# Causal attention's last batch in another order, its last rows finished inside cross attention

## What is computed

```python
# causal attention, 16 heads of 32
q, k, v = jnp.split(jnp.einsum('bsd,de->bse', x, Wqkv), 3, axis=-1)
q = _layernorm_scale_only(q, q_ln_scale)
k = _layernorm_scale_only(k, k_ln_scale)
...
scores = jnp.where(causal, NEG_INF, scores)
attn = jax.nn.softmax(scores, axis=-1)
ctx = jnp.einsum('bhst,bthd->bshd', attn, v)
out = jnp.einsum('bsd,de->bse', ctx.reshape(B, S, D_MODEL), out_W)
...
x = _layernorm(x + _L1_attn_ref(...))
# cross attention, 8 heads over the 256 rows, keys and values from ctx_2048
x = _layernorm(x + _L1_xattn_ref(x, ctx_2048, ctx_2048, L1_xattn_gamma))
x = _layernorm(x + _L1_ffn_ref(...))
```

## Time and profile before

| | us |
|---|---|
| median of 3 runs | 1987.14 (1986.0 to 1990.6) |
| the profiled execution | 1987.22 |
| its span, first to last instruction | 1985.4 |

### The profile page before, as it was taken

The page is one execution under the profiler, slowest core; times in us unless marked ns, Lnnn a source line. Parts: engine busy times, 40 slices in busy tenths (PEclk is TensorE's granted clock), DMA queues, the critical chain, the costliest instruction groups (busy, mean ns, idle before and its releaser), DMA issues. The chain is left out here.

```text
span 1985.4 us, 33011 instructions
## 1 busy us (share of the span) xinstructions
PE 1808.2 (91%) x12256; PEld 1482.3 (75%) x12256; DVE 1218.6 (61%) x2266; ACT 936.8 (47%) x2405; POOL 360.0 (18%) x405
## 2 busy tenths in 40 slices
PE   6989999999998799999999996889999679999976
PEld 5878999998896578888888886677777455656554
DVE  3446444444445775555555533688888668887857
ACT  2225333333334443333333322566667569989845
POOL 0000000000003111111112000233333414243225
PEclk9989999999999899999999998999999789999989
DMA  3023000000014231011111002100011556765432
GB/s 109 33 91 101 22 22 22 1 22 22 22 38 122 75 101 48 17 43 48 29 35 40 17 26 91 54 12 33 33 54 43 121 161 168 172 167 152 107 107 85
DMA packets 84125, 132.46 MB, mean 67 GB/s; under 512 B 9384, under 2 KB 25384, under 8 KB 83968
## 3 DMA queue, kind: packets, MB, share of 16 engines
q1 hardware_dynamic: 83968, 130.36, 23.2%
HBM read 75.72 MB, written 21.05 MB: 49 GB/s over the span
## 5 line engine op out<-in xcount | busy, mean ns | idle before, releaser
L2287 DVE TENSOR_REDUCE e_nb<-e_s_ps 128x2 f32<-128x1024 f32 x128 | 155.7, 1217 | 57.3 <-PE e_s_ps L2359 57.3
L2241 ACT ACTIVATE e_p<-e_s_ps,e_nb 128x512 f32<-128x512 f32 x256 | 175.5, 701 | 19.8 <-DVE e_nb L2287 19.5
L1710 ACT ACTIVATE p<-p,nb,rq 128x128 f32<-128x128 f32 (+1 forms) x256 | 136.9, 541 | 92.9 <-DVE nb L1811 92.9
L894 PE MATMUL yp<-ccy,toep 128*128 128x288 f32 x600 | 159.2, 413 | 5.8 <-ACT ccy L876 4.0
L2369 PE MATMUL e_t_ps<-ident,e_p 128*128 128x128 f32 x1024 | 144.4, 277 | 18.6 <-ACT e_pT L2249 9.9
L2369 PEld LDWEIGHTS e_t_ps<-ident,e_p 128*128 128x128 f32 x1024 | 114.1, 141 | 57.1 <-issue 47.5
L80 PE MATMUL q_ps<-a_xt_hi,wq_hi 128*128 128x256 f32 x512 | 151.8, 297 | 4.1 <-DVE wo_lo L112 4.1
L1231 DVE SCALAR_TENSOR_TENSOR hm<-gu_ps,us_col,sg 128x256 f32<-128x256 f32 x88 | 42.3, 481 | 176.9 <-ACT sg L1120 176.9
L82 PE MATMUL q_ps<-a_xt_hi,wq_lo 128*128 128x256 f32 x512 | 146.2, 286 | 0.0
L81 PE MATMUL q_ps<-a_xt_lo,wq_hi 128*128 128x256 f32 x512 | 145.9, 285 | 0.0
L527 ACT ACTIVATE ex<-ex 128x512 f32<-128x512 f32 x64 | 40.5, 632 | 213.9 <-DVE ex L590 213.9
(11 more groups left out here) (316 smaller groups left out, 5190.6 us busy)
## 6 DMA issues: line engine op xcount, KB each, us to landing
x_after<-n_r SPq DMA_DIRECT2D x16, 512.0 KB, 3.0
toep<-padded_kernels SPq DMA_DIRECT2D x32, 256.0 KB, 3.6
qs<-e_xh SPq DMA_DIRECT2D x64, 128.0 KB, 2.5
qs<-e_xl SPq DMA_DIRECT2D x64, 128.0 KB, 2.5
ks<-e_ch SPq DMA_DIRECT2D x64, 128.0 KB, 2.5
ks<-e_cl SPq DMA_DIRECT2D x64, 128.0 KB, 2.5
x<-x_after SPq DMA_DIRECT2D x9, 512.0 KB, 4.6
x<-in_x SPq DMA_DIRECT2D x8, 512.0 KB, 4.0
```

What stands on the lines that cost most here:

```text
L894: last = pe.matmul(yp[:, lo % 2, 0:NCOL], self.toep[h % 2][:, (lo - li) * P:(lo - li + 1) * P], self.ccy(h)[:, li, 0:NCOL], start=(li == 0 ...
L1710: act.activation(p[n % 3][:, h, part[t]], p[n % 3][:, h, part[t]], ACT.Exp, bias=nb[i][:, t, h:h + 1], scale=rq[u][:, t:t + 1], accum_out= ...
L2241: act.activation(pr[i][:, a, :], s_ps[i][:, a, :], ACT.Exp, bias=nb[i][:, a:a + 1], accum_out=sums[t][:, j, q:q + 1]).then_inc(e_done, 1)
L2287: dve.tensor_reduce(nb[i][:], s_ps[i][:], AX.X, ALU.max, negate=True).then_inc(nb_done, 1)
```

## The change

1. c_hi, x_hi and scale_x of FirstBatch move to step 27, c_lo and x_lo to step 28. stack takes a list of heads: heads 0 and 1 are stacked in SP's turn of batch 6, ahead of store(5) and residual(6); heads 2 and 3 in that of batch 7, ahead of store(6).
2. In the last batch ScalarE's two copies (copy_pt) come before exps(n, 0), and VectorE's copy between the first maxima and reciprocals(n - 1, 1). TensorE's order becomes the turns of n - 2, scores(n + 1), values(n - 2). output(6, 0) comes behind values(28), in step 30, ahead of the turns of step 31; output(6, 1) between the turns and the values of step 31.
3. The output of batch 7 is made by group of heads (output_of_group(7, k), 6 matmuls for both halves): group 0 before values(30), group 1 before values(31), groups 2 and 3 behind.
4. The residual of batch 7 is taken from the x tile in SBUF, which is also where the result is made. Residual, statistics, power, apply and store of batch 7 move into cross attention (class LastRows): residual before VectorE's loop, statistics at m = 1, apply at m = 4, power behind GpSimd's first memset, the store on SP behind the load of batch 1; SP waits for it behind the experts' loads.
5. In cross attention the banks e_v_ps and e_m_ps take the places of the two output banks of causal attention, TensorE waits for the residual sums before it first writes them, and turn_context and context of batch 0 move into the loop, to m = 3 and m = 5.

```diff
@@ FirstBatch
-    def stack(self, sp):
+    def stack(self, sp, heads):
         sp.wait_ge(self.xl_done, 1)
         sp.wait_ge(self.cl_done, 1)
-        for j in range(HT):
+        for j in heads:
@@ new class LastRows
+    def bank_read(self, eng, t):
+        eng.wait_ge(self.p_free[t], self.counts[t])
+
+    def residual(self, dve):
+        for t in range(T):
+            dve.wait_ge(self.o_mm, T * B - T + t + 1)
+            dve.tensor_tensor(self.r[:, t, :], self.p_ps[t][:], self.r[:, t, :], ALU.add).then_inc(self.p_free[t], 1)
+
+    def statistics(self, dve):
+        self.norm.statistics(dve, B - 1, [(self.p_free[t], self.counts[t]) for t in range(T)], r=self.r)
...
@@ l1_attention, SP
                         after.load(sp)
+                        after.stack(sp, (0, 1))
                     if b == B - 1:
-                        after.stack(sp)
+                        after.stack(sp, (2, 3))
                     if b:
                         norm.store(sp, b - 1)
+                    if b and b < B - 1:
                         sp.wait_ge(norm.stored, 16 * b)
                         residual(b)
-                norm.store(sp, B - 1)
-                sp.wait_ge(norm.stored, 16 * B)
@@ GpSimd
+                    if n == NG * (B - 1) - 1:
+                        after.scale_x(pool)
                     normalise(n, 0)
...
-                    if b == B - 1 and g == 0:
-                        after.scale_x(pool)
-                    if b == B - 1 and g == 1:
+                    if n == NG * (B - 1):
                         after.x_lo(pool)
                 normalise(NG * B - 1, 1)
                 norm.power(pool, B - 2)
-                norm.power(pool, B - 1)
@@ ScalarE
+                    if b == B - 1:
+                        copy_pt(n - 2, 0)
+                        copy_pt(n - 2, 1)
                     exps(b, u, n, 0)
...
-                    if n >= 2:
+                    if n >= 2 and b < B - 1:
                         copy_pt(n - 2, 0)
                         copy_pt(n - 2, 1)
...
-                    if b == B - 1 and g == 0:
+                    if n == NG * (B - 1) - 1:
                         after.c_hi(act, (p_mm, 6 * B))
-                    if b == B - 1 and g == 1:
                         after.x_hi(act)
@@ VectorE
                     maxima(b, u, n, 0)
+                    if b == B - 1:
+                        copy_pt(n - 2)
                     if n:
                         reciprocals(n - 1, 1)
...
-                    if b == B - 1 and g == 1:
+                    if n == NG * (B - 1):
                         after.c_lo(dve)
                 last = NG * B - 1
+                lo_out(last - 2)
+                copy_pt(last - 1)
                 reciprocals(last, 1)
-                lo_out(last - 2)
                 statistics(B - 2)
-                copy_pt(last - 1)
-                norm.apply(dve, B - 2)
                 lo_out(last - 1)
                 copy_pt(last)
+                norm.apply(dve, B - 2)
                 lo_out(last)
-                for t in range(T):
-                    residual(B - 1, t)
-                statistics(B - 1)
-                norm.apply(dve, B - 1)
@@ TensorE
+                def output_of_group(b, k):
+                    u = b % 2
+                    pe.wait_ge(ol_done, NG * b + k + 1)
+                    for t in range(T):
+                        if k == 0:
+                            p_bank(t)
+                        ts = slice(t * P, (t + 1) * P)
+                        last = three_pass(pe, p_ps[t][:], oh[u][:, k, ts], ol[u][:, k, ts],
+                                          wo[0][:, k, :], wo[1][:, k, :], k == 0, k == KT - 1)
+                        if k == KT - 1:
+                            last.then_inc(o_mm, 1)
...
+                b, u, last = B - 1, (B - 1) % 2, NG * B - 1
+                scores(b, u, 0, NG * b)
+                for g in range(NG):
+                    n = NG * b + g
                     for m in range(3):
-                        turn_p(n, m, last + 1)
-                    values(n)
-                for t in range(T):
-                    output(B - 1, t)
+                        turn_p(n - 2, m, n + 1)
+                    if g + 1 < NG:
+                        scores(b, u, g + 1, n + 1)
+                    else:
+                        output(b - 1, 1)
+                    values(n - 2)
+                    if g == 2:
+                        output(b - 1, 0)
+                for m in range(3):
+                    turn_p(last - 1, m, last + 1)
+                output_of_group(b, 0)
+                values(last - 1)
+                for m in range(3):
+                    turn_p(last, m, last + 1)
+                output_of_group(b, 1)
+                values(last)
+                output_of_group(b, 2)
+                output_of_group(b, 3)
+        return LastRows(norm, xb[(B - 1) % 2], p_ps, o_mm, p_free, [residual_count(B - 1)] * T)
@@ l1_cross
+        FIRST_TURNS = (3, 5)
@@ SP
                 residual(0, 0)
+                last_rows.store(sp)
                 sp.wait_ge(c_turned, 2)
                 load(2, 0)
                 experts.load(sp)
+                last_rows.wait_stored(sp)
@@ ScalarE
+                        if first and m in FIRST_TURNS:
+                            context(0, 0, FIRST_TURNS.index(m))
-
-                context(0, 0, 0)
-                context(0, 0, 1)
@@ VectorE
                         maxima(b, m)
+                        if first and m == 1:
+                            last_rows.statistics(dve)
+                        if first and m == 4:
+                            last_rows.apply(dve)
...
+                last_rows.residual(dve)
                 over_batches(dve, body, tail)
@@ TensorE
                     if part == 0:
+                        if b == 0 and t == 0:
+                            last_rows.bank_read(pe, 0)
...
+                        if first and m in FIRST_TURNS:
+                            if m == FIRST_TURNS[0]:
+                                last_rows.bank_read(pe, 1)
+                            turn_context(0, 0, FIRST_TURNS.index(m))
-
-                turn_context(0, 0, 0)
-                turn_context(0, 0, 1)
```

More of the change, by code:

```diff
@@ L1509, in qkvo_weights, with __init__, power, apply @@
         [blocks_of(wout, k, 2, slice(0, D)) for k in (0, 2)]
+class LastRows:
+    def __init__(self, norm, r, p_ps, o_mm, p_free, counts):
+        self.norm, self.r, self.p_ps, self.o_mm, self.p_free, self.counts = norm, r, p_ps, o_mm, p_free, counts
+    def bank_read(self, eng, t):
[6 more added lines that the diff above has]
+        self.norm.statistics(dve, B - 1, [(self.p_free[t], self.counts[t]) for t in range(T)], r=self.r)
+    def power(self, pool):
+        self.norm.power(pool, B - 1)
+    def apply(self, dve):
+        self.norm.apply(dve, B - 1, r=self.r)
+    def store(self, sp):
+        self.norm.store(sp, B - 1, r=self.r)
+    def wait_stored(self, sp):
+        sp.wait_ge(self.norm.stored, 16 * B)
 def l1_attention(core, ahead, after, x, y, q_scale, k_scale):
@@ L2024, in _ @@
                 for b, u, g, n in steps():
+                    if b == B - 1:
+                        break
                     scores(b, u, g, n)
@@ L2046, in _, with l1_cross @@
                         values(n - 2)
-                last = NG * B - 1
-                for n in (last - 1, last):
+                b, u, last = B - 1, (B - 1) % 2, NG * B - 1
+                scores(b, u, 0, NG * b)
+                for g in range(NG):
+                    n = NG * b + g
                     for m in range(3):
-                        turn_p(n, m, last + 1)
-                    values(n)
-                for t in range(T):
-                    output(B - 1, t)
-def l1_cross(core, ahead, experts, first_batch, x, ctx_in, y):
+                        turn_p(n - 2, m, n + 1)
[17 more added lines that the diff above has]
+        return LastRows(norm, xb[(B - 1) % 2], p_ps, o_mm, p_free, [residual_count(B - 1)] * T)
+def l1_cross(core, ahead, experts, first_batch, last_rows, x, ctx_in, y):
     nc = core.nc
@@ L2080, in l1_cross @@
         gcol, scale = first_batch.gcol, first_batch.scale
+        v_ps = pb("e_v_ps", [P, D])
+        m_ps = pb("e_m_ps", [P, D])
         s_ps = [pb(f"e_s_ps{i}", [P, 2, D]) for i in range(2)]
         t_ps = [pb(f"e_t_ps{i}", [P, LB, P]) for i in range(2)]
-        v_ps = pb("e_v_ps", [P, D])
-        m_ps = pb("e_m_ps", [P, D])
         s = lambda n: core.sem("e_" + n)
@@ L2187, in _ @@
                 experts.zero(pool)
+                last_rows.power(pool)
                 def scale_x(b, u):
@@ L2399, in body @@
                 def body(b, u, first, last):
-                    used[0] = 2 if first else 4 * b + 1
+                    used[0] = 0 if first else 4 * b + 1
                     for m in range(STEPS):
@@ L2790, in decoder @@
         first_batch = FirstBatch(core, to_cross, gamma)
```

(4 more changed lines are left out.)

## The result

The changed kernel took 1978.04 us (median of 5, 1975.02 to 1981.39) against 1987.31 us before. The ratio is 0.9944, with a 95% interval from 0.9934 to 0.9955: 11.1 us less by the ratio, 9.3 by the medians. The forecast was 1973.7 us, in a range of 1969 to 1981. Measured again in a later job (r1) the ratio was 0.9957 (0.9944 to 0.9971), 8.8 us by the medians, so the gain is about 9 to 11 us where 13.5 were forecast. The time lies inside the stated range, but outside the bounds of the main case (1971.5 to 1976.5).

What follows compares the result with a forecast made beforehand. In causal attention's last batch no engine is full; a chain through three engines, the tail and cross attention's start lose time. 5.3 + 7.3 + 2.6 - 1.0 - 0.7 = 13.5 us off 1987.2 gives 1973.7, range 1969 to 1981.

Steps and rivals of the forecast that it cites:

- main case: The forecast's own sum without the rivals: 1973.7 us, bounds 1971.5 to 1976.5, chance 0.60.
- The steps: Last batch of causal attention: mask of step 31 comes 3.4 us earlier, but the chain is worth 0 within 1 us.
- The tail: End of causal attention, output by groups: TensorE ends at 1585.5 instead of 1590.8 us, gain 5.3 us.
- The border and the start of cross attention: Residual from SBUF and no store at the block's end gain 7.3 us; earlier first maxima gain 2.6 us.
- Cross attention's loop: Cross attention's first steps: two context copies on ScalarE cost 1.0 us, VectorE's statistics 0.7 us (bounds 0 and 3.0).
- SP in cross attention: SP reaches stack(1) about 16 us after the first maxima; with 9 us of cover it costs nothing.
- rival D: Saved time is lost later as cross attention's first batch waits for loads or stacks: 1985.5 us, chance 0.04.
- a shift that shrinks after the first batch: Sign that the forecast is wrong: the time gained by cross attention shrinks after its first batch; no size given.
- rival A: Last batch's steps gain nothing, attention end gains 2, statistics and apply cost 3 us: 1979.3 us, chance 0.20.
- B: Full TensorE clock from step 31 on and in cross attention's first steps: 1971.2 us, chance 0.13.
- C: Low TensorE clock stays in last batch and first of cross attention; 1994 us with 20 us of such work, chance 0.03.
- The shared port: Step 28: c_lo on VectorE could meet GpSimd's power(5) or x_lo, at up to 1 us more.

Runs made afterwards that it cites:

- e7: The changed kernel with the last batch's four steps back in the order of the kernel before; 1980.8 us, ratio 0.9968.
- e4: The changed kernel with the output of batch 6 also made by group of heads, spread over steps 28 to 31; 1974.8 us, ratio 0.9931.
- e5: The changed kernel with experts' loads earlier, batch 2's roundings later, batch 6's output by group, one head stacked in SP's batch 6 turn; 1971.3 us.

## Why the prediction was right, and where it was not

**The steps.** Forecast: mask of step 29 unmoved (9.0 us), 3.4 us gained by the mask of step 31. Measured 8.7 us and 3.05 us; step 29 took 8.5 us and not 7.8. VectorE's wait for the turns of step 31 was to be about 5 us; it was 4.13. That step 31 gives the gain back is shown by e7. The cover that hid c_hi and x_hi held: the masks of steps 27 and 28 stand as far apart as before.

**The tail.** Forecast 5.3 us; the last output starts 1588.03 - 1542.41 = 45.6 us after the mask of step 28, against 1590.39 - 1540.41 = 50.0: 4.4 us. The range of the text began at 4.8. The term was too large by 0.9, and the place is the start of this tail: the second exps of step 31 came 33.8 us after the mask of step 28 (1576.22) and before 32.9 (1573.29), 0.9 us later and not at the same place. What follows them was right: 12.0 us forecast, 12.2 measured to the end of the last output matmul.

**The border and the start of cross attention.** Forecast 7.3 + 2.6. From the last output matmul to the first maxima it is 1589.96 - 1588.03 = 1.9 us now and was 11.96: 10.0 us. Right, to 0.1 us.

**Cross attention's loop.** Forecast a loss of 1.0 + 0.7. From the first maxima to the exps of m = 10 it took 22.34 us against 21.72, so 0.6 us were lost, 1.1 less than I charged. From the exps of m = 2 to those of m = 10 it is 17.27 us against 16.36, 0.9 us for the two context copies, nearly as charged. The error stands in the first steps: the exps of m = 2 start 5.1 us after the first maxima, statistics included, and before 5.4. TensorE's granted clock is 1.00 there in the changed kernel (1591 to 1601) and 0.50 before (1595 to 1605), so what statistics cost by themselves is not shown. By m = 10 the gain was 13.8 us, where the sum says 13.5. That agreement is partly luck: the tail was too large by 0.9 and the loop's loss by 1.1.

**SP in cross attention: the step that failed.** The text said that stack(1) comes later (about 16 us; it was 17.4), and that this costs nothing because the next batch's scores have 9 us of cover. The scores did have it; by the text's own numbers (35 less 16 and 8) it was 11 us. But stack(1) has a second reader of its completion: ScalarE's rounding of batch 2, which may write the tile only when all 32 DMAs have read it, and which stands at m = 0 in ScalarE's queue. That wait was in the trace of before with 0.48 us, so its cover was not 9 us but less than none. The question "who waits for this queue" was asked of those who read its result and not of those who overwrite its source. The part of rival D that was right is its mechanism; its place and price were wrong (5.1 us lost by a delay of 2.6; the text had asked for a delay of 21 us to lose 12, which by its own sum makes 1985.7 and not 1985.5 us). The text had named its sign, a shift that shrinks after the first batch. The 8.7 us measured and the 5.1 us of the step make 13.8, beside the sum's 13.5. The forecast range holds the result only because it was drawn to take in rival A, whose loss to statistics and apply the traces don't show.

**The rivals.** A (the steps gain nothing and cross attention loses more, 1979.3 us) is nearest in time but not in kind: its loss was to come from statistics and apply. B (a full clock from step 31 on) came in part: the clock was full from 1570 on, 2 us into output(6, 0), and held at the border, but those 2 us are the place where B's attention end was to gain. C did not come: 1.00 from 1570 to 1589. What the text held against C was misread, though: in the trace of before the clock doesn't come back within 10 us of each fall, it is low from about 1553 to 1570 and from about 1594 to 1607.

**The shared port.** The text weighed that c_lo at its new place could meet power(5). VectorE's c_lo and GpSimd's first instruction of power(5) in the changed kernel:

```profile
1550.02 1.19 DVE L1494 TENSOR_TENSOR e_cl<-ring,e_ch 128x1024 fp32r<-128x1024 f32 x1
...
1550.18 1.08 POOL L231 TENSOR_TENSOR n_rstd<-n_mv,eps 128x2 f32<-128x2 f32 x1 [0.53 <-DVE n_mv L225]
```

c_lo ran from 1550.02 to 1551.21; this addition on 128x2, 0.20 us at 1582.00 for batch 6, ended at 1551.26. The Trainium skill (SBUF — State Buffer, section "Who interferes with whom") says that a VectorE instruction with two SBUF inputs contends with a GpSimd instruction that reads SBUF, and the trace agrees. It cost GpSimd 0.9 us and VectorE nothing. x_lo stands behind it in GpSimd's queue and ended at 1554.34, where SP's first stack issue follows at 1554.37, so a part of residual(6)'s cover went here.

## What to carry to other kernels

When a queue is delayed, look for everyone who waits for its DMAs: the readers of what they write, and the engines that want to overwrite what they read from. A wait of half a microsecond in the old trace marks a place without any cover, where each further microsecond counts in full; here more was lost than the wait itself, and TensorE's clock fell behind it. Work that fills idle time in a chain of waits (the output by group in e4) can be worth more than a shorter chain: the clock stayed full with it, and the first maxima came 2.0 us earlier. A shorter chain in front of a queue that is full anyway (the turns behind output(6, 0)) brought nothing.

## What the runs showed of the hardware

The code ahead of the mask of step 28, nearly all of it unchanged, took 1538.9 to 1545.8 us in the traces. The mean granted clock up to there is 0.98 in all of them, so this spread isn't explained. The clock's falls are a term of their own at the level of some microseconds. The wait of 3.2 us in batch 1 was followed by transposes at 1.94 us instead of 1.06. With three groups of six output matmuls in the gaps of the steps, about 4 us of work at the full clock, the granted clock was 1.00 from 1545 to 1570 in both kernels that have them (e4 and e5), where the changed kernel had 0.53. I had not expected so little work, moved into the gaps, to go with such a difference.
